# A two-layer graph attention kernel: score masks and the linear part of the scores by TensorE, the running minimum one step earlier

## The reference

```python
h = layer_norm(x); xl = h @ Wl + bl; xr = h @ Wr + br
e = leaky_relu(xl[src] + xr[dst], 0.2)
score = einsum('ehd,hd->eh', e, att)
ex = exp(score - segment_max(score, dst)[dst])
alpha = ex / (segment_sum(ex, dst)[dst] + 1e-16)
g = segment_sum(xl[src] * alpha, dst) + gat_b
x = x + g @ proj_W + proj_b
x = x + gelu(layer_norm(x) @ W1 + b1) @ W2 + b2
```

## Time and profile before

| | us |
|---|---|
| median of 3 runs (2282.32 to 2284.36) | 2283.58 |
| profiled execution, its own time | 2276.5 |
| its span | 2274.8 |
| first layer: first gather to last gather | 109.65 to 1121.81 |
| second layer: first gather to last gather | 1209.14 to 2203.51 |

### The profile page before, as it was taken

The page is one execution under the profiler, slowest core; times in us unless marked ns, Lnnn a source line. Parts: engine busy times, 40 slices in busy tenths (PEclk is TensorE's granted clock), DMA queues, the critical chain, the costliest instruction groups (busy, mean ns, idle before and its releaser), DMA issues. The chain is left out here.

```text
span 2274.8 us, 76766 instructions
## 1 busy us (share of the span) xinstructions
PE 1820.8 (80%) x22500; PEld 1285.0 (56%) x22500; DVE 1806.9 (79%) x8130; ACT 1368.8 (60%) x3471; POOL 1573.6 (69%) x1663
## 2 busy tenths in 40 slices
PE   2478888888888888888864788888878888888884
PEld 1145566665665665665642565665656656566663
DVE  6757888888888888888854788888888888888874
ACT  3444666666666666666652466666666666666664
POOL 2677777777777777777505777777777777777750
PEclk6878999999999999999976999999999999999995
DMA  4455556556556556555404555555555555555540
GB/s 105 157 158 145 150 152 157 154 150 156 150 150 161 155 146 158 149 152 153 110 23 132 150 146 147 150 152 150 150 147 155 151 149 149 148 154 151 149 109 9
DMA packets 227679, 320.66 MB, mean 141 GB/s; under 512 B 47889, under 2 KB 157574, under 8 KB 227270
## 3 DMA queue, kind: packets, MB, share of 16 engines
q0 software_dynamic: 75072, 208.30, 36.1%
q1 hardware_dynamic: 152198, 107.47, 15.9%
HBM read 295.61 MB, written 19.99 MB: 139 GB/s over the span
## 5 line engine op out<-in xcount | busy, mean ns | idle before, releaser
L973 POOL DMA_INDIRECT rows<-table,src_t x1564 | 1521.0, 973 | 495.1 <-issue 453.4
L1188 ACT ACTIVATE lz<-psum 128x512 f32<-128x512 f32 x782 | 465.6, 595 | 377.6 <-PE psum L1093 189.9
L1090 PE MATMUL psum<-ident,rows 128*128 128x128 f32 x3128 | 529.9, 294 | 56.7 <-DMA rows<-table,src_t 56.3
L1265 ACT ACTIVATE ex<-hold_s,peak 128x128 f32<-128x128 f32 x782 | 272.1, 396 | 410.4 <-DVE peak L1346 409.5
L1163 PE MATMUL psum<-rows,wgt 128*32 128x129 f32 x6256 | 260.8, 284 | 277.6 <-DVE acc L1436 277.0
L1090 PEld LDWEIGHTS psum<-ident,rows 128*128 128x128 f32 x3128 | 351.4, 146 | 210.2 <-issue 140.9
L1436 DVE SCALAR_TENSOR_TENSOR acc<-acc,keep,psum 128x129 f32 x782 | 272.5, 348 | 190.9 <-issue 115.7
L1163 PEld LDWEIGHTS psum<-rows,wgt 128*32 128x32 f32 x6256 | 159.3, 111 | 364.8 <-issue 216.9
L1074 PE MATMUL psum<-lz,att_w 128*32 128x128 f32 x6256 | 345.4, 294 | 0.0
L1093 PE MATMUL psum<-oh,xrw 96*128 96x256 bf16 x1564 | 312.9, 282 | 0.0
L1313 DVE TENSOR_SCALAR diff<-row_no,cyc_t 128x64 bf16<-128x64 f32 x1564 | 290.8, 258 | 0.0
(11 more groups left out here) (253 smaller groups left out, 2130.8 us busy)
## 6 DMA issues: line engine op xcount, KB each, us to landing
xrw<-xr_split SPq DMA_DIRECT2D x782, 48.0 KB
relb<-rel_d SPq DMA_DIRECT2D x194, 192.0 KB
rows<-table,src_t POOLq DMA_INDIRECT x1564
xr_split<-split SPq DMA_DIRECT2D x50, 192.0 KB, 1.9
table<-row SPq DMA_DIRECT2D x50, 130.0 KB, 2.0
x_mid<-x SPq DMA_DIRECT2D x25, 64.0 KB
xo<-x_mid SPq DMA_DIRECT2D x25, 64.0 KB
xo<-in_x_dram SPq DMA_DIRECT2D x24, 64.0 KB
```

Source lines behind the costliest of these rows:

```text
L973: pool.indirect_dma_start(rows[:, u % ROWS, t, :, :].rearrange("p h c -> p (h c)"), None, s["tables"][layer][0:NP, :], bass.IndirectOffset ...
L1090: pe.matmul(z[:, o:o + P], rows[:, u % ROWS, t, h, 0:D], s["ident"][:, :], is_transpose=True, start=(h == 0 and t == 0), stop=False, skip_ ...
L1188: act.activation(lz[:, u % M, :], ps[u % M][:, :], ACT.Relu).then_inc(lz_ready, 1)
L1265: m = act.activation(ex[:, (u + 1) % (2 * M), :], hold_s[:, place(u), :], ACT.Exp, bias=peak[:, place(u + 1):place(u + 1) + 1], scale=-1.0)
```

## The change

- Destinations go to DRAM a second time (`cyc_d`), and a second DMA per four units brings them to the upper 32 partitions of `relb`, whose lower 96 hold what they held. The comparison for the one-hot matrices runs over 128 partitions, with a second operation that subtracts `less` (0 below, 1 in the upper 32), so that the upper part is 0 where the edge belongs to the slot and -1 elsewhere. `oh` gets six places in place of four.
- `differ`, `bases`, `row_no` and `cyc_t` go. In their place TensorE does, per unit, four matmuls of 128 rows by 32 columns in float32 (the linear part broadcast as weights, the identity as moving data) and two of 128 rows by 64 columns in bfloat16 (`mask_w` by the upper part of `oh`), ahead of its wait for the relu.
- `lowest` handles step i-2 in step i, that is the step in which ScalarE copies these scores; the exponentials, their turning, their copy, the sums, `added` and all node work come one step earlier. The wait of the one-hot matrices is now for the scores of step i-2.
- In `setup` the turning of the destinations (seven transposes and copies, one cast, three DMAs, five VectorE operations) gives way to four VectorE operations on the units' layout and one DMA.

```diff
             def score(u):
                 g = u // M
                 out = scores(g)[:, u % M * P:u % M * P + P]
+                if u % M == 0:
+                    hold(pe, held, g - 1)
+                for t in range(K):
+                    for h in range(H):
+                        o = t * HW + h * W
+                        pe.matmul(out[o:o + W, :], rows[:, u % ROWS, t, h, D + 1:RC].to_broadcast([P, W]), s["ident"][:, :],
+                                  start=True, stop=False, skip_group_check=True)
+                for t in range(K):
+                    pe.matmul(out[t * HW:t * HW + HW, :], s["mask_w"][:, :], oh[:, u % (3 * M), t * P:t * P + P],
+                              start=False, stop=False, skip_group_check=True)
                 pe.wait_ge(lz_ready, u + 1)
-                if u % M == 0:
-                    pe.wait_ge(base_ready, g + 1)
-                    hold(pe, held, g - 1)
-                pe.matmul(out, base[:, u % (2 * M), :, :].rearrange("p c w -> p (c w)"), s["ident"][:, :],
-                          is_transpose=True, start=True, stop=False, skip_group_check=True)
...
-                old = behind(i - 6)
+                old = behind(i - 5)
                 if old:
-                    pe.wait_ge(wgt_ready, i - 5)
+                    pe.wait_ge(wgt_ready, i - 4)
...
# ScalarE
-                old = behind(i - 3)
+                old = behind(i - 2)
                 for u in old:
-                    act.wait_ge(max_ready, i - 2)
+                    act.wait_ge(max_ready, i - 1)
...
# VectorE
-                    m = v.tensor_scalar(oh[:, u % (2 * M), :], relb[:, u % RING, :], s["win_col"][0:3 * W, 0:1], None,
-                                        ALU.is_equal)
+                    m = v.tensor_scalar(oh[:, u % (3 * M), :], relb[:, u % RING, :], s["win_col"][:, 0:1],
+                                        s["less"][:, 0:1], ALU.is_equal, ALU.subtract)
...
-                if of_step(i - 3):
-                    lowest(i - 3)
-                if of_step(i):
-                    bases(i)
+                if of_step(i - 2):
+                    lowest(i - 2)
...
                 if of_step(i + 1):
-                    hold(v, z_ready, (i - 1) * M + M)
+                    hold(v, score_ready, i - 1)
                     one_hot(i + 1)
-                    hold(v, base_ready, i)
-                    differ(i + 1)
...
-    return min(behind_of(t * TILE + 20), NO - 1) + 9
+    return min(behind_of(t * TILE + 20), NO - 1) + 8
```

More of the change, by code:

```diff
@@ L301, in _ @@
             const(pool.iota(third_i[:, :], [[0, 1]], base=0, channel_multiplier=171))
-            const(pool.iota(g["row_no0"][:, :], [[0, H], [1, W]], base=0, channel_multiplier=0,
-                            allow_small_or_imprecise_dtypes=True))
+            const(pool.memset(g["less"][0:3 * W, :], 0.0))
+            const(pool.memset(g["less"][3 * W:P, :], 1.0))
+            const(pool.memset(mask_f[:, :], 0.0))
+            for h in range(H):
+                const(pool.affine_select(out=mask_f[3 * W:P, h * W:h * W + W], in_=mask_f[3 * W:P, h * W:h * W + W],
+                                         compare_op=ALU.not_equal, fill=-BIG, base=0, pattern=[[-1, W]],
+                                         channel_multiplier=1))
+            const(pool.tensor_copy(g["mask_w"][:, :], mask_f[:, :]))
             const(pool.memset(g["sel"][:, :, :, :], 0.0))
@@ L429, in _ @@
                            ).then_inc(order_ready, 1)
-            for j in range(2 * TJ):
+            for j in range(TJ):
                 act.wait_ge(turned, j + 1)
-                to = src_t[:, j, :] if j < TJ else dst_t[:, (j - TJ) * P:(j - TJ) * P + P]
-                act.copy(to, ps[3 + j % 2][:, 0:P]).then_inc(copied, 1)
+                act.copy(src_t[:, j, :], ps[3 + j % 2][:, 0:P]).then_inc(copied, 1)
             act.wait_ge(averaged, 1)
@@ L454, in _ @@
             pe.matmul(ps[2][:, 0:1], g["ones"][:, :], uns[:, :], start=True, stop=True).then_inc(order_spread, 1)
-            pe.wait_ge(src_cast, 2)
-            for j in range(2 * TJ):
+            pe.wait_ge(src_cast, 1)
+            for j in range(TJ):
                 if j >= 2:
                     pe.wait_ge(copied, j - 1)
-                pe.transpose(ps[3 + j % 2][:, 0:P], src_f[:, j, :] if j < TJ else dst_df[:, j - TJ, :],
-                             g["ident"][:, :]).then_inc(turned, 1)
+                pe.transpose(ps[3 + j % 2][:, 0:P], src_f[:, j, :], g["ident"][:, :]).then_inc(turned, 1)
 def hold(eng, semaphore, value, gate=None):
@@ L1092, in project @@
                 for h in range(H):
-                    m = pe.matmul(z[:, h * UE:h * UE + UE], xrw[:, place(u), h * D:h * D + D], oh[:, u % (2 * M), :],
+                    m = pe.matmul(z[:, h * UE:h * UE + UE], xrw[:, place(u), h * D:h * D + D], oh[0:3 * W, u % (3 * M), :],
                                   start=False, stop=(h == H - 1), skip_group_check=True)
@@ L1385, in next_pass @@
                                 ).then_inc(moved, 1)
[L1386 to L1387 removed]
             def next_tables():
[L1391 removed]
+                v.wait_ge(moved, 7)
                 v.tensor_scalar(hop[:, :], s["at_s"][:, :], SLOTS - 0.5, float(-SLOTS), ALU.is_ge, ALU.mult
@@ L1425, in _ @@
             one_hot(0)
-            differ(0)
             slots = []
             for i in range(END):
-                old, here = behind(i - 7), slots
+                old, here = behind(i - 6), slots
                 if old:
-                    v.wait_ge(sums_ready, i - 6)
-                    hold(v, added, i - 7)
+                    v.wait_ge(sums_ready, i - 5)
+                    hold(v, added, i - 6)
                 for u, j in zip(old, here):
```

145 lines of the change are left out of this document (59 added, 86 removed).

## The result

| | before | changed |
|---|---|---|
| median, us | 2283.97 (2282.32 to 2285.32) | 2586.67 (2573.07 to 2600.24) |
| profiled execution's span | 2274.8 | 2583.9 |

The ratio is 1.1326 (1.1265 to 1.1386). The forecast was 2445 us in a range of 2320 to 2525: the side was right, the size too small by 142 us, and the time lies above the range.

The account below looks back on a forecast made before the run. GpSimd's gathers set the pace at 5.0 us a step; the moved step's chain would make it 5.6. 179 steps x 0.6 x 2 = 215 us, less 54, gives 2437 us, 2445 as median; range 2320 to 2525.

Parts of the forecast that it names:

- GpSimd's pitch as the pace: GpSimd's gathers come every 1.25 us, a floor of 5.0 us a step or 976 us a layer.
- The matmuls' price: On TensorE, six matmuls come and one goes per unit: 0.6 us more a step, bounds 0.4 and 1.1.
- a: First of eight TensorE steps in a row: work 4.65 us after the change, wait before it 0.64 us.
- e: Fifth of eight TensorE steps in a row: work 5.89 us after the change, no wait before it.
- h: Last of eight TensorE steps in a row: work 4.38 us after the change, no wait before it.
- The moved step's chain: ScalarE's relu and copy, VectorE's minimum, register loads and additions, TensorE's sums: 5.0 to 7.6 us, covered by one TensorE step.
- Work and waits are 39.8 + 5.5 = 45.3 us: TensorE's work plus waits in eight steps after the change: 5.66 us a step against 5.15, taken as 5.6.
- d: Fourth of eight TensorE steps, behind the square-root step: work 4.17 us after the change, wait before it 1.95 us.
- g: Seventh of eight TensorE steps, behind the MLP step: work 6.38 us after the change, wait before it 2.03 us.
- Rival C: ScalarE's round delays relus and GpSimd loses lead, or matmuls cost 1.1 us: 5.85 a step, 2534 us; chance 0.13.
- Rival A: At the gathers' wait, GpSimd keeps the pace and the stalls go: faster, 2225 us; chance 0.09.

Follow-up runs that it names:

- f1: The changed kernel with the moved step undone and the new matmuls kept: 2227.68 us, 0.9767 of the kernel before.
- f3: The changed kernel with ScalarE's copy to hold_s moved right behind the first relu: 2218.03 us, 0.9736 of the kernel before.
- g4: The changed kernel with the early copy to hold_s and the register loads ahead of the minimum: 2222.16 us, 0.9749 of the kernel before.
- f4: The changed kernel with sixteen useless matmuls per eight steps put into TensorE's long waits: 2457.89 us, 1.0778 of the kernel before.
- e1: The changed kernel with the moved step undone, run on the slower kind of chip: 1.1259 of the kernel before.

## Why the prediction was right in kind and wrong in size

1. **GpSimd's pitch as the pace: right.** f1, f3 and g4 come to 982 to 985 us a phase on the floor of 976.
2. **The matmuls' price: right, slightly high.** In kinds of step that had no half clock in either kernel TensorE's work grew by 0.53 to 0.57 us (a from 4.05 to 4.59, e from 5.27 to 5.82, h from 3.75 to 4.28, in layer 1); the forecast took 0.6. TensorE's own work in eight steps, a mean over a layer, is 39.1 and 38.4 us in f1, where half clock is rare; the forecast had 39.8. At the change to 64 columns, for which no row stood, the weight loads of L1071 have 174.9 us of issue before them, 0.22 us a unit; how much of that lengthens a step no run separates. The Trainium skill, TensorEngine Tiling (Array Packing), Key Properties, says that a change of tiling mode drains TensorE. This idle time fits that, and no run here shows more.
3. **The moved step's chain: right in place.** In the changed kernel relu to the copy's end is 0.86 us in light steps, 2.57 in the MLP step and 2.48 in the one with the square root (taken: 0.86, 2.57 and 2.5); minimum 1.59 to 1.78 (1.65); `peak` to addition 1.25, 2.47 and 2.19 (1.4, 2.25 and 2.0); additions to sums 0.99 (1.01).
4. **The term that failed is "Work and waits are 39.8 + 5.5 = 45.3 us", and in it the works of d and g, 4.17 and 6.38 us.** The means over the two layers are 47.9 and 49.4, or 6.0 and 6.2 a step where the sum went on with 5.6. The forecast's works were taken from eight steps at clock 1.00 and set behind waits of 2 us, as if they would always run as fast there. They don't: d takes 5.24 and 5.87 us in the two layers, g 7.17 and 8.27, where at full clock they take 4.08 and 6.36. Where no half clock falls into eight steps, 776.91 to 823.05, they took 46.14 us. The waits were mis-sized by less: 6.3 and 7.0 us of idle time in eight steps against 5.5. The forecast's phases were 976 + 179 x 0.6 = 1083 us; f4, whose waits are filled, has 1095.5 and 1088.6; the changed kernel 1138.7 and 1171.0. So some 126 of the 142 us missed are the clock, as far as f4 shows it, and about 17 a chain slightly longer than summed. What is left, some 5 us outside the phases and a median 1 us above the profiled execution in place of 7, nearly cancels.
5. **Could it have been seen?** The clock of 0.96 stood in the earlier trace rows, and it meant 85 and 88 us of half clock with waits of 277 us. Rows 4, at clock 1.00 throughout, showed none of it. A forecast that lengthens waits has to ask what the clock does behind them. Rival C reached 2534 us by another road and still fell short.
6. **Rival A** had the weight 0.09 and lost, rightly: f1 shows that it needs the step undone, f3 that with the step kept one copy placed elsewhere is enough. The forecast did not see that so small an edit separates the two outcomes.

## What to carry to other kernels

When a loop over engines gets longer than the step that covers it, find the operation that starts it, and ask what stands ahead of that on its engine only by the order of the program: here the place of one copy of 0.37 us, behind ScalarE's second relu and node work, was the difference between 1.133 and 0.974. When a forecast adds waits to TensorE, work out a second sum with the steps behind them priced from rows at half clock: here some 6 us in place of 4.1, in 33 of 42 steps d. Of two parts sold as one change, time each alone: one was worth -2.3%, the other +18%, and the two did not add up.

## What the runs showed of the hardware that was not expected

- Work added into waits made a kernel faster: 16 matmuls per eight steps, -129 us, mean clock 0.99 in place of 0.94 and 0.90. A stretch at half clock began within the second of two pauses of 1.02 and 1.28 us; after like waits the same step ran at half clock 12 times of 21 in layer 1 and 21 of 21 in layer 2.
- The kernel before takes 2279 us on one chip and 2833 to 2914 us on another, the changed one 2587 and 3355 to 3361. A ratio from one kind (0.977 for f1) can be 1.126 on the other (e1).
- Two register loads just ahead of an addition cost it 0.7 us of delay in light steps (`peak` to addition, 1.25 to 0.55), time in which VectorE executes nothing.
